# Opening the banks of the key maxima with the masks instead of the products

## The reference

```python
# cross-attention, q = layernorm(x), k = v = ctx
scores = einsum('bhqd,bhkd->bhqk', qh, kh) / sqrt(dh)
merged = where(causal == 1, causal, pad)          # key j > query i, or key padded
scores = where(merged == 1, -inf, scores)
attn = softmax(scores, axis=-1)
out = einsum('bhqk,bhkd->bhqd', attn, vh)
x = x + tanh(g_xattn) * (out @ W.T + b)
# feed-forward: shared SwiGLU expert + top-2 of 8 experts
x = x + tanh(g_ffn) * ffn(layernorm(x))
```

## Time and profile before

| what | value |
|---|---|
| timed runs, median of 3 | 1208.58 us (1202.61 to 1209.3) |
| the profiled execution, its own time | 1207.33 us |
| its span, first to last instruction | 1205.5 us |
| TensorE matmul busy | 1130.7 us, 94% |
| TensorE weight load busy | 902.5 us, 75% |
| VectorE busy | 805.9 us, 67% |
| ScalarE, GpSimd busy | 467.9 us (39%), 446.0 us (37%) |
| mean granted TensorE clock | 0.986 |

### The profile page before, as it was taken

The page is one execution under the profiler, slowest core; times in us unless marked ns, Lnnn a source line. Parts: engine busy times, 40 slices in busy tenths (PEclk is TensorE's granted clock), DMA queues, the critical chain, the costliest instruction groups (busy, mean ns, idle before and its releaser), DMA issues.

```text
span 1205.5 us, 22268 instructions
## 1 busy us (share of the span) xinstructions
PE 1130.7 (94%) x7475; PEld 902.5 (75%) x7475; DVE 805.9 (67%) x1777; ACT 467.9 (39%) x722; POOL 446.0 (37%) x576
## 2 busy tenths in 40 slices
PE   2778999999999999999999899999999699999997
PEld 1456777777777777787777677788888588888886
DVE  5466686676676676776766776446644488777676
ACT  3455555555555546545555442223322111111110
POOL 3122334335235236245235422200000566566654
PEclk9989999999999999999999999999999799999999
DMA  5947576566657647656664411468653554454541
GB/s 132 215 100 146 114 122 137 114 108 130 132 99 139 137 107 123 138 116 104 141 131 78 106 36 44 147 224 273 204 190 129 162 164 153 144 154 148 159 148 47
DMA packets 114720, 162.62 MB, mean 135 GB/s; under 512 B 37964, under 2 KB 79342, under 8 KB 114608
## 3 DMA queue, kind: packets, MB, share of 16 engines
q1 hardware_dynamic: 102964, 123.19, 45.2%
q0 software_dynamic: 11648, 38.03, 10.4%
HBM read 74.72 MB, written 51.58 MB: 105 GB/s over the span
## 4 chain that ended last, share of the span: by engine, by line
PE 76%; issue 9%; DVE 6%; POOL 5%; DMA 2%; ACT 2%; POOLq 0%; another core or an unknown queue 0%; DVEq 0%; ACTq 0%
PE ps L720 15%; PE ps L766 12%; PE ps L665 9%; PE ps L768 6%; PE ps L682 6%; PE ps L573 4%; PE ps L585 4%; PE ps L616 3%; PE ps L545 3%; PE ps L751 3%; PE ps L540 3%; POOL tab_dram L1392 2%; PE ps L568 2%; DMA regr<-regr 1%; PE ps L594 1%
## 5 line engine op out<-in xcount | busy, mean ns | idle before, releaser
L766 PE MATMUL ps<-regr,gh 128*128 x600 | 221.4, 406 | 2.4 <-issue 2.2
L833 ACT ACTIVATE Pt<-ps,pbias 77x1024 f32<-77x1024 f32 x128 | 141.6, 1106 | 193.3 <-PE ps L573 186.9
L768 PE MATMUL ps<-regr,gl 128*128 x600 | 169.9, 283 | 0.1
L1301 POOL DMA_INDIRECT yt<-y_dram,Pt x75 | 77.7, 1036 | 200.8 <-issue 200.8
L766 PEld LDWEIGHTS ps<-regr,gh 128*128 128x128 f32 x600 | 113.7, 190 | 26.5 <-issue 3.3
L1134 DVE TENSOR_REDUCE mneg<-ps 128x8 f32<-128x616 f32 x128 | 101.6, 794 | 42.3 <-PE ps L545 40.1
L926 ACT ACTIVATE gh<-ps 128x512 fp32r<-128x512 f32 x75 | 44.0, 598 | 212.3 <-PE ps L751 107.6
L768 PEld LDWEIGHTS ps<-regr,gl 128*128 128x128 f32 x600 | 113.9, 190 | 0.8 <-issue 0.8
L1368 POOL TENSOR_TENSOR x<-x,regf 128x512 f32<-128x512 f32 x32 | 41.2, 1287 | 191.3 <-DMA x<-in_x 191.3
L665 PE MATMUL ps<-x2h,winh 128*128 128x512 f32 x256 | 110.5, 432 | 0.5 <-DVE OHR L1041 0.5
L1405 POOL DMA_INDIRECT out<-ot,Pt x75 | 77.7, 1036 | 82.2 <-DVE ot L1260 51.9
(11 more groups left out here) (197 smaller groups left out, 2628.7 us busy)
## 6 DMA issues: line engine op xcount, KB each, us to landing
regr<-regr SPq DMA_DIRECT2D x96, 256.0 KB, 5.9
y_dram<-Pt SPq DMA_DIRECT2D x64, 256.0 KB, 2.1
regf<-in_x SPq DMA_DIRECT2D x32, 256.0 KB, 2.8
x<-in_x SPq DMA_DIRECT2D x32, 256.0 KB, 7.1
y_dram<-res SPq DMA_DIRECT2D x32, 256.0 KB, 2.1
regr<-regr SPq DMA_DIRECT2D x96, 77.0 KB, 4.7
x_dram<-x2h SPq DMA_DIRECT2D x14, 512.0 KB, 2.9
x_dram<-x2l SPq DMA_DIRECT2D x14, 512.0 KB, 3.7
```

The costliest lines, as they stand in the source:

```text
L766: e.matmul(o, gh2[:, k % 3, fc, :], w2v[:, bass.ds(val, 1), fc, :, :].rearrange("p o h d -> p (o h) d"), start=fc == 0, stop=False, skip_g ...
L768: m = e.matmul(o[:, 0, :], gl2[:, k % 3, fc, :], w2v[:, bass.ds(val, 1), fc, 0, :].rearrange("p o d -> p (o d)"), start=False, stop=fc == ...
L833: e.activation(Pt[0:K, 4 * k:4 * k + 4, :].rearrange("k (n j) t -> k n (j t)", n=2), bank_of["sc", b, k][0:K, :, :], ACT.Exp, bias=pbias[: ...
L1301: e.indirect_dma_start(yt[k % RY][:, :], None, y, bass.IndirectOffsetOnAxis(ap=rt[:, k, 0:1].bitcast(I32), axis=0), bounds_check=NT, oob_i ...
```

## The change

In a group of the maxima the two mask matmuls are issued first and open the two banks (start=True: they overwrite). The two products of 64 rows come after them and are added, and the last product closes the group and increments `mm`. The wait for `first`, which only group k = 0 has, stays ahead of the mask matmuls and is so ahead of the products as well. Nothing else changes: operands, sizes and counts are the same.

```diff
@@ -536,14 +536,14 @@
                     e.wait_ge(sem, v)
                     o = bk[:, :, 0:4 * K].rearrange("p q (h k) -> p q h k", h=4)
 
-                    for q in range(2):
-                        e.matmul(o[:, q], xTh[64 * q:64 * q + 64, h, c, t * P:(t + 1) * P],
-                                 Kbd[64 * q:64 * q + 64, ks, g, c, :, :], start=True, stop=False)
                     if k == 0:
                         e.wait_ge(s["first"], b + 1)
                     for q in range(2):
-                        m = e.matmul(o[:, q], identb[:, :], (pad[:, b, :] if t else first[:, h, :]).unsqueeze(1).broadcast_to([P, 4, K]),
-                                     start=False, stop=True)
+                        e.matmul(o[:, q], identb[:, :], (pad[:, b, :] if t else first[:, h, :]).unsqueeze(1).broadcast_to([P, 4, K]),
+                                 start=True, stop=False)
+                    for q in range(2):
+                        m = e.matmul(o[:, q], xTh[64 * q:64 * q + 64, h, c, t * P:(t + 1) * P],
+                                     Kbd[64 * q:64 * q + 64, ks, g, c, :, :], start=False, stop=True)
                     m.then_inc(s["mm"], 1)
```

## The result

The changed kernel takes 1216.13 us in the median of 20 runs, the kernel before 1209.41 in the median of 20 on the same chips. The ratio is 1.0051, with a 95% interval of 1.0031 to 1.0072: 6.2 us slower (3.7 to 8.7); the two medians themselves lie 6.7 us apart. The forecast was 1210.3 in a range of 1203 to 1218, that is +3.0: the sign and the range hold, the size is half of what came.

The account below looks back on a forecast made before the run. TensorE, busy 94% of the span, was taken as the bound. 30 groups at 0.09 and 98 at 0.015 gave +4.2 us; less some 1.2, +3.0 on 1207.3 made 1210.3, range 1203 to 1218.

Parts of the forecast that it names:

- the split exposes the load: Maxima groups: weight loads are exposed where the array goes from 128 rows to halves of 64 and back.
- point 2: Products behind the masks: still 0.34 us, so a change of 0, bounded by 0.13 and 0.47.
- point 3: cauT pair behind the products: 0.26 us instead of 0.14, +0.12; net +0.01 to +0.02 a group.
- point 4: Projection behind group k = 2: up to 1.63 us instead of 1.42, +0.20; net +0.09 a group.
- k = 2 as the dear place: Group k = 2, followed by the projection's f32 weights: 30 blocks at +0.09 us, 2.7 us together.
- Point 1: Masks, now behind a matmul of 128 rows: their load hides, 0.26 us instead of 0.37, -0.11 a group.
- deduction of 1.2 us: Taken off the +4.2 us: at most 0.5 for cauT pairs waiting anyway at k = 0, 0.8 absorbed off TensorE's chain.
- The waits: Earlier wait for `first` costs nothing; `mm` 0.11 us earlier returns at most 0.6 us, counted within what is absorbed.
- A: Rival: the products' weight load hides behind the masks, products 0.13 us, total 1189 us; chance 0.06.
- B: Rival: the products, now adding, no longer run side by side, 0.128 us more a group, total 1223; chance 0.08.
- D: Rival: the way back after the products costs 0.21 us for all followers, total 1218 us; chance 0.08.
- C: Rival: nothing to see, no switch cost or the loss absorbed at starved places, 1207 to 1208 us; chance 0.18.

Follow-up runs that it names:

- e1: One mask matmul before and one after the two products in every group, against the kernel before: 1200.67 us against 1198.6, ratio 1.0015 (0.9998 to 1.0032).
- e2: New order only for group k = 2, old order for the others, against the kernel before: ratio 1.0017 (0.9994 to 1.0040).
- e3: New order only for groups k = 0, 1 and 3, old order for k = 2, against the kernel before: ratio 1.0017 (0.9998 to 1.0037).
- e4: Kernel before with products on 128 rows, using zero-padded copies that ScalarE makes before xTh; products still first: 1212.1 us, ratio 1.0101 against the kernel before.
- e5: Products on 128 rows by the same zero-padded copies, but masks first as in the changed kernel: 1213.26 us, ratio 1.0119 against the kernel before.
- e6: Changed kernel with the projection one slot later in the hand-written order: 1210.92 us, ratio 1.0097 against the kernel before.

## Why the prediction was right, and where it was not

- **Where the time goes (the split exposes the load): right.** The load of whatever stands behind a switch is what is exposed. The products still take 0.34 behind bf16 masks (point 2), cauT 0.26 behind the products (point 3), the projection 1.61 (point 4), as written. The time exposed goes with the length of the load, to 0.01 us: 0.107 for identb's load of 0.098 us, 0.122 for cauT's of 0.117, 0.198 for the projection's of 0.188 (medians). e1, e2 and e3 show that the loss follows the load behind the switch; e4 and e5 that it vanishes with the switch.
- **k = 2 as the dear place: right.** A quarter of the groups, half of the loss (e2, e3). The Trainium skill, page "TensorE: Matmul & The Clock Gate", section "LDWEIGHTS (loading the stationary operand)", puts a load at columns divided by 1.2, by estimate 107 ns for 128 columns of any type. By that k = 2 would have cost next to nothing; the trace doesn't agree, with 0.188 us for f32 against 0.098 for identb, and the measured rows decided rightly.
- **Point 1 is the term that was mis-sized.** I put the masks at 2 x 0.13 = 0.26, "their load hides, as their second one does now". They take 0.28 to 0.29, outside the 0.26 to 0.27 that the prediction had named as the mark of being right. Behind f32 weights the load of identb begins with its own matmul (308.41), not ahead of it, and 0.02 us are left over. Over 128 groups that is 2.6 us, nearly as much as the forecast's whole +3.0. The trace of before had a row that hinted at it: the rank matmul L696, 96 columns in bf16 with weights of 128 x 128 right after L665 in f32, takes 0.06 where 96 columns are 0.04.

```profile
604.37 0.70 PE ps L665 x3
605.07 0.06 PE ps L696
```

- **The deduction of 1.2 us was wrong.** 0.8 of it was a fifth of the sum, taken off because a fifth of the chain isn't TensorE's; the other part was for cauT pairs that wait anyway. In the stretch where I could count, nothing was absorbed: working time grew by 4.9 us, and idle time didn't shrink (9.0 and 8.9 before, 9.7 and 9.3 after). A share of a chain is no share of what gets absorbed: that needs waits of TensorE which shrink as its work grows, and these didn't. 3.0 + 2.6 + 1.2 = 6.8; with the measured medians in place of the rounded terms the sum is 6.2, as measured.
- **The range held by its width.** The mechanism and the sign were right, but both errors of size pointed the same way and made the sum half of what came; 15 us of range, set by the rivals and the scatter of the runs, covered that.
- **The waits: right.** Nobody waits for `first` at its earlier place. TensorE's waits for the maxima, 5.5 us in 5, are 6.0 in 6: the earlier `mm` bought nothing.
- **The rivals.** A and B (0.13 or 0.47 for the products) are out by the row of 0.34. D (0.21 for all) holds only where the load is f32: 0.20 for the projection, 0.12 for cauT. C is out by the interval. With +0.51% the result lies on the bound of what I had called the same; the 0.19 for slower was low for a forecast whose own terms were uncertain by as much as its size.

## What to carry to other kernels

Where matmuls of different array tilings are mixed, count the switches, and for each the weight load of the instruction behind it: reordering only pays if it puts a shorter load there, or merges two switches into one. But look at the engine's idle time and granted clock before you book the gain: e4 and e6 worked less, as planned, and lost more than that in waits, in a late start and at the lower clock. Zero-padding the operand of a small product to the full array cost one more stream of 0.13 us and saved 0.16 us net a group, but only with the additional copies placed where no queue waits for what stands behind them. And a sum of small terms over 128 groups is as good as its smallest term: 0.02 us, rounded away, came to nearly the size of the forecast.

## What I had not expected of the hardware

Two products of 64 rows that flow side by side were slower than two full ones in a row (0.34 and 0.11 behind them, against 0.28). bf16 weights of 128 columns right behind f32 ones add some 0.02 us to the stream even with no switch, in the changed kernel, in e1 and in e4 alike, while cauT, 77 columns in bf16, takes 0.14 for 0.13 behind the projection and the masks alike. The step from 64 to 20 rows costs one switch (0.98 for L650 in e6). And a wait of TensorE of some 2 us can cost more than itself: where the granted clock fell to 0.50 for 3.4 us at it, another 1.4 us went (the changed kernel's second trace), in some executions and not in others.
